# Cross-attention on one core: scores of four heads at once in every tile, and another split and order of the first stores

## The chip, the cores and the metric

One core of one Trainium2 chip. The metric is the time of one execution in microseconds on the device; a run's time is that of its slowest core, here the only one. "Span" is the time from the first to the last instruction in the profile of one execution.

## The reference, cut to what matters

```
def _L0_xattn_ref(tgt, memory, Wq, Wk, Wv):          # tgt, memory: (32, 512, 512) f32; NH = 16, dk = 32
    q = (tgt @ Wq.T).reshape(B, N, NH, dk).transpose(0, 2, 1, 3)
    k = (memory @ Wk.T)...                           # in the same way
    v = (memory @ Wv.T)...
    scores = jnp.einsum('bhqd,bhkd->bhqk', q, k) * (1.0 / np.sqrt(dk))
    probs = jax.nn.softmax(scores, axis=-1)
    att = jnp.einsum('bhqk,bhkd->bhqd', probs, v).transpose(0, 2, 1, 3).reshape(B, N, D)
    return tgt + att[0]
```

Only att of the first of the 32 sequences is used, and it is added to all 32. So the attention is computed once (512 queries, 512 keys, 16 heads of width 32), while 33.5 MB of x are read and 33.5 MB of sums are written.

## The kernel before

The 512 query rows are four tiles of 128. A row of x in SBUF is laid out in pairs: x is seen as two halves J of 256 rows, and partition p of a half holds rows 2p and 2p+1, r = 0 and 1. Tiles 0 and 1 are r = 0 and 1 of half 0, tiles 2 and 3 those of half 1. The 32 sequences are 16 groups g of two, and `slots` has 17 places of one group and one half (1 MB each). Half 0 is loaded into 16 of them while the weights and keys are prepared, group 0 of half 1 into the last. Every other group of half 1 (`slot_of`) goes into a place from which half 0's result has been stored.

**Adding and storing.** Tile 0 comes out in two units: FIRST is its first eight heads (columns 0 to 255), SECOND its other eight. Groups below SPLIT are added and stored in halves, once for each unit, those from SPLIT on as a whole row, in SECOND. Tile 1 is the unit ROW_1. Tiles 2 and 3 are added together at the end (`add_whole`, L698, on VectorE; L270 on GpSimd), one slot of 1 MB at a time. GpSimd has the odd groups of each unit and VectorE the even ones. VectorE's adds are written out by hand between the operations of the heads (L706 to L731, L751 to L780). All DMAs are issued by SyncE from one queue in the order L207 to L247: loads, FIRST's stores in the order of g, SECOND's stores in the order of g, BY_ROWS reloads of row 0 (`reload_row`, L191), then ROW_1's stores alternating with reloads, then `store_slot` for 16 groups. A store waits for its add (L182, L187), a reload for its slot's stores (L193). The stores of L188 need att of tiles 2 and 3, thus the end of the whole attention.

**The attention of one tile.** For every head h: TensorE makes the scores (3 passes, f32 split in a high and a low fp32r part) into PSUM bank h % 4; VectorE takes the negated maximum (`head_max`, L656); ScalarE takes the exponential with its sum (`exponent`, L574) into `probs[h % 2]`; TensorE turns it in four 128x128 transposes (`turn_probs`, L366) into PSUM bank 4 + h % 2; ScalarE copies that to `probs_t[h % 6]` (`copy_transposed`, L581). For every four heads TensorE multiplies with v (`weigh_values`, L375, 32 matmuls), VectorE copies the result (`copy_att_t`, L668) and inverts the sums (L661). At a tile's end `turn_back` (L387, L394) turns att back and `normalize` (L672) scales it.

A score matmul uses 32 of the 128 rows of the array, so the matmuls of different heads of a group of four go to different rows. `scores` (L347) issues pass by pass over the heads that it is given. In tile 0, and for heads 0 to 3 of every tile, these are four (`score_group`, L355, 12 matmuls), otherwise two (`score_pair`, L362, 6 matmuls). A group waits until all four heads before it have their exponentials, since the four banks are the same; a pair waits until the pair two before it has. One semaphore step, after the last matmul, releases all heads of one call.

Each engine works in the order in which its instructions are written. For tiles 1 to 3 these orders are `heads` of TensorE (L398), of ScalarE (L589) and of VectorE (L706). Between the heads of tile j they also prepare tile j+1: x is turned (`turn("x0_t")`), copied as a high part by ScalarE and a low part by VectorE (`empty`, L644), multiplied with wq in four chunks of three matmuls (`query_chunk`, L306), copied by ScalarE (`empty("q")`, L569), turned again (`turn("q_t")`) and copied in two parts. All of this uses PSUM bank 7, which the product with v uses too, and so chunk 0 waits for att of heads 0 to 3 to be copied away, and the turn of q for heads 4 to 7 (`pe.wait_ge(att_t_ready, ...)`). After tile 0 come `keep_warm` transposes (L459) on the identity.

## Time and profile before

| | |
|---|---|
| median of 3 runs | 195.05 us (194.85 to 198.45) |
| the profiled execution, its own time | 193.7 us |
| its span | 191.9 us |
| mean granted TensorE clock | 0.886 of full speed |
| busy: TensorE / VectorE / ScalarE / GpSimd | 129.7 / 113.5 / 96.3 / 63.6 us |
| moved by DMA | 71.5 MB, mean 373 GB/s |
| scores of heads 0 to 3 start in tile 0, 1, 2, 3 | 32.70, 67.68, 92.90, 118.95 us |
| last product with v starts | 142.40 us |
| first store of the last half is issued | 148.24 us |

Times in the profile are from the span's start. The profiled execution took 1.8 us more than its span. L with a number is a line of the kernel, "x12" a count of instructions, SPq SyncE's queue. A matmul's shown length includes the time until its result is there, so that matmuls in a row overlap in the timeline; the chain of waits shows how long they hold the engine.

### The profile page before, as it was taken

Reading aid. Unit: us, or ns where it says so; the run is one execution under the profiler, and the core shown is the slowest. Engines: PE = TensorE matmul, PEld = TensorE weight load, DVE = VectorE, ACT = ScalarE, POOL = GpSimd, SP = SyncE. Lnnn points to the kernel's source line nnn. Section 1 sums busy time; section 2 is a strip of 40 time slices with the busy share of each in tenths; the row PEclk is TensorE's granted clock in tenths of the full one; section 3 lists DMA queues with packets and bytes.
Section 4 is the critical chain, followed back from the end, with each engine's and each line's share of the span. In section 5 each row is a group of like instructions: output and inputs, shape, how many; then the busy total and the mean of one; then the engine's idle time right before and its main releaser. Section 6 shows DMA issues by size and latency. Waiting matters only on the chain.

```text
span 191.9 us, 3371 instructions
## 1 busy us (share of the span) xinstructions
PE 129.7 (68%) x1252; PEld 95.4 (50%) x1252; DVE 113.5 (59%) x169; ACT 96.3 (50%) x225; POOL 63.6 (33%) x33
## 2 busy tenths in 40 slices
PE   6999999999779967998879998888871000000000
PEld 6878786766547744766656765665650000000000
DVE  0546637653476578857599867945518999940000
ACT  2525553864677259868788879798860000000000
POOL 1000000000066599200079996000007999900000
PEclk9999999999999999999999999999999555555555
DMA  5999999999999793789999999999999999999997
GB/s 215 359 374 417 408 410 410 410 405 408 412 361 329 232 333 126 279 318 348 395 385 400 365 397 408 401 406 406 418 413 414 394 409 404 406 406 408 406 408 304
DMA packets 28976, 71.52 MB, mean 373 GB/s; under 512 B 1696, under 2 KB 6816, under 8 KB 28832
## 3 DMA queue, kind: packets, MB, share of 16 engines
q1 hardware_dynamic: 28960, 71.31, 96.5%
q8 instruction: 10, 0.16, 0.3%
q14 instruction: 6, 0.05, 0.1%
HBM read 37.75 MB, written 33.55 MB: 372 GB/s over the span
## 4 chain that ended last, share of the span: by engine, by line
PE 50%; ACT 16%; DVE 13%; issue 8%; DVEq 2%; POOL 0%; ACTq 0%; POOLq 0%
PE bank L371 11%; DVE slots L703 10%; ACT probs L578 8%; PE bank L351 7%; PE bank L329 6%; PE bank L306 6%; ACT probs_t L586 6%; PE bank L340 6%; PE bank L382 5%; PE bank L298 5%; PE bank L454 2%; DVE neg_max L658 2%; DVEq L58 2%; PE bank L394 1%; ACT ctx_t L572 1%
## 5 line engine op out<-in xcount | busy, mean ns | idle before, releaser
L264 POOL TENSOR_TENSOR slots<-slots,att_rows 128x1024 f32<-128x1024 f32 (+1 forms) x22 | 40.4, 1876 | 76.4 <-DVE att_rows L684 76.4
L578 ACT ACTIVATE probs<-bank,neg_max 128x512 f32<-128x512 f32 x64 | 45.1, 705 | 13.7 <-DVE neg_max L658 12.8
L658 DVE TENSOR_REDUCE neg_max<-bank 128x1 f32<-128x512 f32 x64 | 41.6, 680 | 15.7 <-PE bank L351 15.6
L371 PE MATMUL bank<-ident,probs 128*128 128x128 f32 x256 | 40.1, 282 | 8.7 <-ACT probs L578 7.4
L586 ACT COPY probs_t<-bank 128x512 f32<-128x512 f32 x64 | 37.7, 593 | 11.9 <-PE bank L371 10.3
L371 PEld LDWEIGHTS bank<-ident,probs 128*128 128x128 f32 x256 | 27.9, 140 | 23.3 <-ACT probs L578 19.1
L270 POOL TENSOR_TENSOR slots<-slots,att_rows 128x2048 f32<-128x2048 f32 x5 | 22.5, 4531 | 27.1 <-DVE att_rows L684 27.1
L351 PE MATMUL bank<-k_t,x_q 32*128 32x512 f32 x192 | 24.1, 424 | 0.9 <-issue 0.6
L703 DVE TENSOR_TENSOR slots<-slots,bank 128x2048 f32<-128x2048 f32 x11 | 24.3, 2279 | 0.0
L695 DVE TENSOR_TENSOR slots<-slots,bank 128x512 f32<-128x512 f32 (+1 forms) x20 | 18.7, 944 | 0.1
L382 PE MATMUL bank<-probs_t,v 128*32 128x128 f32 x512 | 17.3, 276 | 1.1 <-ACT probs_t L586 0.7
L351 PEld LDWEIGHTS bank<-k_t,x_q 32*128 32x128 f32 x192 | 12.3, 183 | 7.2 <-issue 5.4
L382 PEld LDWEIGHTS bank<-probs_t,v 128*32 128x32 f32 x512 | 13.0, 109 | 5.1 <-issue 2.2
L670 DVE COPY att_t<-bank 128x128 f32<-128x128 f32 x16 | 4.6, 289 | 17.4 <-PE bank L382 17.3
L306 PE MATMUL bank<-wq_t,x_q 128*128 128x512 f32 x48 | 14.3, 416 | 0.1
L578 ACT ACTIVATION_READ_ACCUMULATOR probs<-bank,neg_max 128x1 f32 x64 | 13.7, 214 | 0.0
L329 PE MATMUL bank<-ctx_t,wk_t 128*128 128x512 f32 x48 | 13.3, 409 | 0.4 <-ACT ctx_t L572 0.3
L340 PE MATMUL bank<-wv_t,ctx_t 128*128 128x512 f32 x48 | 13.3, 409 | 0.3 <-issue 0.3
L340 PEld LDWEIGHTS bank<-wv_t,ctx_t 128*128 128x128 f32 x48 | 8.3, 188 | 2.9 <-issue 1.1
L329 PEld LDWEIGHTS bank<-ctx_t,wk_t 128*128 128x128 f32 x48 | 8.3, 189 | 2.4 <-ACT ctx_t L572 0.6
L306 PEld LDWEIGHTS bank<-wq_t,x_q 128*128 128x128 f32 x48 | 8.0, 189 | 1.6 <-issue 0.7
L653 DVE TENSOR_TENSOR wk_t<-bank,wk_t 128x512 fp32r<-128x512 f32 x4 | 2.8, 692 | 10.1 <-ACT wk_t L572 10.1
(41 smaller groups left out, 89.5 us busy)
## 6 DMA issues: line engine op xcount, KB each, us to landing
slots<-in_x_dram SPq DMA_DIRECT2D x21, 1024.0 KB, 14.3
out_dram<-slots SPq DMA_DIRECT2D x16, 1024.0 KB, 13.3
slots<-in_x_dram SPq DMA_DIRECT2D x22, 512.0 KB, 9.0
out_dram<-slots SPq DMA_DIRECT2D x22, 512.0 KB, 7.0
out_dram<-slots SPq DMA_DIRECT2D x20, 256.0 KB, 3.1
ctx_raw<-in_ctx_dram SPq DMA_DIRECT2D x1, 1024.0 KB, 4.9
wq_raw<-in_L_xattn_Wq_dram SPq DMA_DIRECT2D x1, 1024.0 KB, 9.3
wv_raw<-in_L_xattn_Wv_dram SPq DMA_DIRECT2D x1, 1024.0 KB, 12.3
```

The lines of the kernel that those rows point to most:

```text
L264: nc.gpsimd.tensor_tensor(xs, xs, a.unsqueeze(1).to_broadcast([P, BPS, a.shape[1]]), ALU.add).then_inc(added[g], 1)
L270: nc.gpsimd.tensor_tensor(xs, xs, last_att.unsqueeze(1).to_broadcast([P, BPS, ROWS * D]), ALU.add).then_inc(added[g], 1)
L306: last = mm(job_bank("q", j), x0_q[:, j % 2, c, a, :], wq_t[:, c, b, :], start=(c == 0 and (a, b) == PASSES[0]), stop=(c == C - 1 and (a, ...
L329: last = mm(job_bank("k_t", g), wk_t[:, c, a, g * P:(g + 1) * P], ctx_t[:, c, b, :], start=(c == 0 and (a, b) == PASSES[0]), stop=(c == C ...
L340: last = mm(job_bank("v", t), ctx_t[:, c, a, t * P:(t + 1) * P], wv_t[:, c, b, :], start=(c == 0 and (a, b) == PASSES[0]), stop=(c == C - ...
L351: last = mm(bank[:, h % S_BANKS, :], x0_q[rows, j % 2, g, a, :], k_t[rows, g, b, :], start=((a, b) == PASSES[0]), stop=((a, b) == PASSES[-1]))
L371: last = nc.tensor.transpose(bank[:, PT_BANK + h % 2, t * P:(t + 1) * P], probs[:, h % 2, t * P:(t + 1) * P], ident[:, :])
L382: last = mm(att_t_ps[i * DK:(i + 1) * DK, g, :], v[:, t, h * DK:(h + 1) * DK], probs_t[:, (j * HEADS + h) % PT_SLOTS, t, :], start=(t == 0 ...
L578: nc.scalar.activation(probs[:, h % 2, :], bank[:, h % S_BANKS, :], ACT.Exp, bias=neg_max[:, h:h + 1], scale=1.0, accum_out=row_sum[:, h:h ...
L586: nc.scalar.copy(probs_t[:, (j * HEADS + h) % PT_SLOTS, :, :], bank[:, PT_BANK + h % 2, :].rearrange("p (t n) -> p t n", t=T)).then_inc(pr ...
L658: nc.vector.tensor_reduce(neg_max[:, h:h + 1], bank[:, h % S_BANKS, :], AX_X, ALU.max, negate=True).then_inc(max_ready, 1)
L703: nc.vector.tensor_tensor(xs, xs, back.unsqueeze(1).to_broadcast([P, BPS, ROWS * D]), ALU.add).then_inc(added[g], 1)
```

## The change

The stores of FIRST and SECOND go in an order written out by hand (`STORE_ORDER`); twelve groups instead of ten are added and stored in halves; twelve instead of ten have their row 0 reloaded by itself, before ROW_1's stores. `score_pair` goes: heads 4 to 15 of tiles 1 to 3 also have their scores made in groups of four. TensorE's, ScalarE's and VectorE's orders in `heads` are laid out again around this, and VectorE makes four of SECOND's adds instead of three before tile 1's heads.

```
-    SPLIT = 10
-    BY_ROWS = 10
-    DVE_GROUPS = {FIRST: (0, 2, 4, 6, 8), SECOND: (0, 2, 4, 6, 8, 10, 12, 14), ROW_1: (0, 2, 4, 6, 8, 10, 12)}
-    POOL_GROUPS = {FIRST: (1, 3, 5, 7, 9), SECOND: (1, 3, 5, 7, 9, 11, 13, 15),
+    SPLIT = 12
+    BY_ROWS = 12
+    DVE_GROUPS = {FIRST: (0, 2, 4, 6, 8, 10), SECOND: (0, 2, 4, 6, 8, 10, 12, 14), ROW_1: (0, 2, 4, 6, 8, 10, 12)}
+    POOL_GROUPS = {FIRST: (1, 3, 5, 7, 9, 11), SECOND: (1, 3, 5, 7, 9, 11, 13, 15),
                    ROW_1: (1, 3, 5, 7, 9, 11, 13, 14, 15)}
+    STORE_ORDER = {FIRST: (1, 0, 3, 2, 5, 4, 7, 6, 9, 8, 11, 10),
+                   SECOND: (0, 2, 1, 4, 3, 6, 5, 7, 9, 8, 11, 10, 12, 13, 14, 15)}
...
         def scores_through(j, h):
-            if j == 0:
-                return h // HPG + 1
-            return HG + (j - 1) * (PAIRS - 1) + (1 if h < HPG else h // PAIR)
+            return j * HG + h // HPG + 1
...
-            for g in range(SPLIT):
-                store(FIRST, g)
-            for g in range(GROUPS):
-                store(SECOND, g)
+            for unit in (FIRST, SECOND):
+                for g in STORE_ORDER[unit]:
+                    store(unit, g)
...
-            def score_pair(j, pair):
-                pe.wait_ge(exp_ready, j * HEADS + pair * PAIR - PAIR)
-                scores(j, range(pair * PAIR, (pair + 1) * PAIR))
-
...
                 turn_probs(j, 0)
                 turn_probs(j, 1)
-                score_pair(j, 2)
                 turn_probs(j, 2)
+                score_group(j, 1)
                 turn_probs(j, 3)
-                score_pair(j, 3)
-                turn_probs(j, 4)
-                turn_probs(j, 5)
                 if more:
                     emptied(pe, "x0_t", j + 1)
                 weigh_values(j, 0)
-                score_pair(j, 4)
-                turn_probs(j, 6)
+                turn_probs(j, 4)
                 if more:
                     pe.wait_ge(att_t_ready, j * HG + 1)
                     query_chunk(j + 1, 0)
+                turn_probs(j, 5)
+                if more:
+                    query_chunk(j + 1, 1)
+                turn_probs(j, 6)
+                score_group(j, 2)
                 turn_probs(j, 7)
                 if more:
-                    query_chunk(j + 1, 1)
-                score_pair(j, 5)
+                    query_chunk(j + 1, 2)
+                    query_chunk(j + 1, 3)
                 turn_probs(j, 8)
-                if more:
-                    query_chunk(j + 1, 2)
-                turn_probs(j, 9)
-                if more:
-                    query_chunk(j + 1, 3)
-                score_pair(j, 6)
                 if more:
                     raw_queries_out(j + 1)
                 weigh_values(j, 1)
+                turn_probs(j, 9)
                 turn_probs(j, 10)
+                score_group(j, 3)
+                turn_probs(j, 11)
                 if more:
                     pe.wait_ge(att_t_ready, j * HG + 2)
                     turn_queries(j + 1)
-                turn_probs(j, 11)
-                score_pair(j, 7)
                 turn_probs(j, 12)
                 turn_probs(j, 13)
                 if more:
                     emptied(pe, "q_t", j + 1)
                 weigh_values(j, 2)
                 turn_probs(j, 14)
+                if more:
+                    score_group(j + 1, 0)
                 turn_probs(j, 15)
-                if more:
-                    score_group(j + 1, 0)
                 weigh_values(j, 3)
...
             def heads(j):                                    # ScalarE
                 for h in range(HEADS):
                     exponent(j, h)
-                    if h > 0:
+                    if h % HPG > 0:
                         copy_transposed(j, h - 1)
+                    if h % HPG == HPG - 1:
+                        copy_transposed(j, h)
                     if j + 1 < T:
                         if h == 2:
                             empty("x0_t", j + 1)
-                        if h == 10:
+                        if h == 7:
                             empty("q", j + 1)
-                        if h == 11:
+                        if h == 12:
                             empty("q_t", j + 1)
-                copy_transposed(j, HEADS - 1)
...
                 for h in range(HPG, HEADS):                  # VectorE
                     if h % HPG == 0 and h >= 2 * HPG:
                         copy_att_t(j, h // HPG - 2)
+                    if h == HPG and j + 1 < T:
+                        empty("x0_t", j + 1)
+                    head_max(j, h)
                     if h == HEADS - 2 and j + 1 < T:
                         empty("q_t", j + 1)
-                    head_max(j, h)
-                    if h == HPG + 1 and j + 1 < T:
-                        empty("x0_t", j + 1)
...
-            add(SECOND, DVE_GROUPS[SECOND][0])
-            add(SECOND, DVE_GROUPS[SECOND][1])
+            for g in DVE_GROUPS[SECOND][:3]:
+                add(SECOND, g)
             empty("q_t", 1)
-            add(SECOND, DVE_GROUPS[SECOND][2])
+            add(SECOND, DVE_GROUPS[SECOND][3])
             for h in range(HPG):
                 head_max(1, h)
-            heads(1, SECOND, list(DVE_GROUPS[SECOND][3:]))
+            heads(1, SECOND, list(DVE_GROUPS[SECOND][4:]))
```

## Rows read from the trace of the kernel before

**Rows 1.** The page, 40 slices of 4.8 us: granted TensorE clock (tenths), data rate.

```profile
PEclk9999999999999999999999999999999555555555
...
GB/s 215 359 374 417 408 410 410 410 405 408 412 361 329 232 333 126 279 318 348 395 385 400 365 397 408 401 406 406 418 413 414 394 409 404 406 406 408 406 408 304
```

**Rows 2.** Timeline from 143 us: start, length, engine, line, operation, count. The end.

```profile
142.40 1.08 PE L382 MATMUL bank<-probs_t,v 128*32 128x128 f32 x32 [0.68 <-ACT probs_t L586]
...
143.90 0.66 PE L394 MATMUL bank<-ident,att_t 128*128 128x128 f32 x4 [0.42 <-DVE att_t L670]
...
148.24 28.70 SPq L188 DMA_DIRECT2D out_dram<-slots  x16
```

**Rows 3.** Chain of waits: start, length on the engine, what. Tile 2.

```profile
102.96 1.01 PE bank L382 x32
103.97 0.89 PE bank L351 x6
...
106.14 0.44 PE bank L371 x4
106.58 0.69 PE bank L306 x3
```

**Rows 4.** Timeline of tile 0: two score groups in a row.

```profile
39.25 0.97 PE L351 MATMUL bank<-k_t,x_q 32*128 32x512 f32 x12
...
45.76 0.97 PE L351 MATMUL bank<-k_t,x_q 32*128 32x512 f32 x12 [0.32 <-ACT probs L578]
```

**Rows 5.** Timeline at the change from tile 1 to tile 2.

```profile
92.90 0.97 PE L351 MATMUL bank<-k_t,x_q 32*128 32x512 f32 x12
93.00 0.59 ACT L586 COPY probs_t<-bank 128x512 f32<-128x512 f32 x1
...
93.80 1.08 PE L382 MATMUL bank<-probs_t,v 128*32 128x128 f32 x32
...
95.46 0.66 PE L394 MATMUL bank<-ident,att_t 128*128 128x128 f32 x4 [0.58 <-DVE att_t L670]
...
96.39 1.04 PE L371 MATMUL bank<-ident,probs 128*128 128x128 f32 x8
...
97.50 0.69 ACT L578 ACTIVATE probs<-bank,neg_max 128x512 f32<-128x512 f32 x1
...
98.34 0.66 PE L371 MATMUL bank<-ident,probs 128*128 128x128 f32 x4
98.65 0.61 ACT L572 CAST x_q<-bank 128x512 fp32r<-128x512 f32 x1
...
99.12 0.72 ACT L578 ACTIVATE probs<-bank,neg_max 128x512 f32<-128x512 f32 x1
```

**Rows 6.** Timeline at the change from tile 2 to tile 3.

```profile
118.95 0.98 PE L351 MATMUL bank<-k_t,x_q 32*128 32x512 f32 x12
...
119.86 1.08 PE L382 MATMUL bank<-probs_t,v 128*32 128x128 f32 x32
119.97 1.29 DVE L658 TENSOR_REDUCE neg_max<-bank 128x1 f32<-128x512 f32 x2 [1.45 <-PE bank L351]
```

**Rows 7.** Timeline of tile 2: an add, a turn and its copy, the last query chunk.

```profile
103.16 1.21 DVE L695 TENSOR_TENSOR slots<-slots,bank 128x1024 f32<-128x1024 f32 x1
...
104.29 0.28 DVE L670 COPY att_t<-bank 128x128 f32<-128x128 f32 x1
...
104.79 0.66 PE L371 MATMUL bank<-ident,probs 128*128 128x128 f32 x4
...
105.48 0.59 ACT L586 COPY probs_t<-bank 128x512 f32<-128x512 f32 x1 [0.90 <-PE bank L371]
...
109.62 0.93 PE L306 MATMUL bank<-wq_t,x_q 128*128 128x512 f32 x3
```

**Rows 8.** Timeline of tile 1's first heads.

```profile
67.68 0.97 PE L351 MATMUL bank<-k_t,x_q 32*128 32x512 f32 x12 [0.57 <-issue]
...
73.05 0.72 ACT L578 ACTIVATE probs<-bank,neg_max 128x512 f32<-128x512 f32 x1
```

More of the change, by code:

```diff
@@ L32, in cross_attention_add @@
     SLOTS = GROUPS + 1
-    PAIR = 2
-    PAIRS = HEADS // PAIR
     S_BANKS = 4
@@ L446, in heads @@
                 turn_probs(j, 14)
-                turn_probs(j, 15)
                 if more:
                     score_group(j + 1, 0)
+                turn_probs(j, 15)
                 weigh_values(j, 3)
```

## The prediction

> **What bounds the kernel now.** I read the data rate first, then the end of the timeline, then the chain of waits, then the timeline of single heads.
>
> The rate [rows 1] stands near 408 GB/s from the fourth slice to the eleventh and again from about slice 24 on. Between them are eight slices (361, 329, 232, 333, 126, 279, 318, 348) that fall short of 410 by 954 in all, so 954/410 x 4.8 = 11.2 us of transfer time are lost there. This is all that an earlier or better ordered store can win; a part of it is not idle time but slower small pieces.
>
> The end [rows 2] shows a second bound. The last product with v starts at 142.40; 5.84 us later, at 148.24, the first store of the last half is issued. Behind it lie 16 stores of 1 MB, 16.8 MB, which at the 406 GB/s of the last slices take 41.3 us, and the span ends at 191.9. These stores can't start before the attention of all four tiles is done. From 142.40 to the end are 49.5 us that nothing in the change touches. So the attention's chain and the data rate meet at about 148: if only the transfers before it get better, the queue runs dry and waits for the attention; if the attention gets later, the end gets later one for one, and whatever the stores won is lost. The attention decides, and the question is how long tiles 1 to 3 take. Now their score groups start at 67.68, 92.90 and 118.95 [rows 8, 5, 6]: 25.2 us, 26.05 us, and 23.45 us from the last to 142.40.
>
> **The change part by part.**
>
> *Splits and store order.* SPLIT 12 moves two half adds (a half add is two times shorter than the row add of 1.13 us, 103.16 to 104.29 [rows 7]) into tile 0's time, where VectorE waits for TensorE anyway, and two in GpSimd, which waits for att; the order lets the first store go about 1 us sooner and takes away the wait at SECOND's seventh store. I bound the gain for the transfers by 0 and 11.2 us and take 4. On the path that sets the end it is 0, since the attention ends later (below). SyncE's queue has four more issues (two stores, two reloads), about 0.5 us each, long before 148. More small pieces cost transfer time that has become free. Bounds for this part: 0, or 1 us lost. I take 0.
>
> *TensorE's work.* A pair holds TensorE for 0.89 us [rows 3], a group for 0.91 (118.95 to 119.86, [rows 6]). Six pairs a tile become three groups: 6 x 0.89 - 3 x 0.91 = 2.6 us less for TensorE a tile, 7.8 us in three tiles. It counts only where TensorE is what everything waits for.
>
> *The loop that a group makes.* Steps from rows: scores start to first maximum 1.02, two maxima in 1.29, so 0.6 to 0.65 each [rows 6]; exponential to its turn, or to the scores that wait for it, 0.84 (97.50 to 98.34), exponential and a copy on ScalarE 1.15 and a copy 0.47 (97.50, 98.65, 99.12), so an exponential alone 0.68 [rows 5]; turn to copy 0.69 (104.79 to 105.48, [rows 7]); a turn holds TensorE 0.44, a query chunk 0.69, a product with v 1.01 [rows 3]; a copy's start to the product that waits for it 0.80 (93.00 to 93.80, [rows 5]); that product to TensorE's next, through the copy of att, 1.50 (142.40 to 143.90, [rows 2]), of which the copy has 0.28 [rows 7].
>
> With S the start of a group's scores, the new order runs so: the turn of the last head of the group before starts at S+0.91, because it stands behind the scores; its copy at S+1.60; the group's first exponential stands behind that copy, at S+2.07 (its maximum would allow S+1.7); second S+2.75; third, behind the first turn's copy, S+4.5; fourth S+5.7; the next scores S+6.5. So a group takes at least 6.1 (2.93 between its neighbours' exponentials and 3.15 for its own four), and about 6.5 with a product with v in it. Tile 0 works so already and shows 6.51 (39.25 to 45.76, [rows 4]). A pair lets ScalarE go on at 1.15 a head while the next scores are made; a group drains it each time. Four groups are 24.3 to 26 us where tile 3 takes 23.45 now.
>
> *Stall at query chunk 0 (tiles 1, 2).* It now stands before turn 5 and waits for att of heads 0 to 3. That copy stands on VectorE behind the maxima of heads 4 to 7 and two adds: S1 + 1.02 + 4 x 0.60 + 2 x 1.13 + 0.09 (the reciprocal) = S1+5.77; with 0.35 for the copy and the step to TensorE the chunk starts at S1+6.12, turn 5 at 6.81, its copy at 7.50, exponential 7 at 7.97, the next scores at S1+8.8 instead of 6.5. Queued behind the waiting chunk are turns 5 and 6 and with them ScalarE. Cost 2.3 us a tile. Before, a pair of scores and a turn lay in front of the chunk and nothing waited.
>
> *q copied after head 7 (tiles 1, 2).* Chunks 2 and 3 follow turn 7: chunk 3 starts at S2 + 0.91 + 0.44 + 0.69 = 2.04, its result is there 0.93 later (the matmuls of 109.62, [rows 7]), ScalarE's copy of q is at S2+3.0, and exponential 8 stands behind it: S2+3.5 instead of 2.07. Group 2 to group 3 is then 7.8. In group 3 q_t stands between exponentials 12 and 13, but chunk and maxima are in time: 6.3 to the next tile's scores.
>
> *Change of tile.* Scores of the next tile now come before turn 15. Turn 15's copy is at S0+1.60, the last product with v at S0+2.4 (it was S0+0.91), turned back 1.50 later, at S0+3.9, and from there as now: turn 0 at +0.93 (95.46 to 96.39), exponential 2 at +1.11, x0's copy and exponential 3 at +1.15 and +0.47 [rows 5], S1 = S0+8.4. In tile 3 there is no x0: S0+7.4.
>
> *Sum.* Tile 1, whose start has no such change (scores at 67.68, exponential 3 at 73.05, S1 at 73.9 [rows 8]): 6.2 + 8.9 + 7.8 + 6.3 = 29.2, now 25.2: +4.0. Tile 2: 8.4 + 8.8 + 7.8 + 6.3 = 31.3, now 26.05: +5.3. Tile 3: 7.4 + 6.5 + 6.4 + 7.5 (to its last product with v) = 27.8, now 23.45: +4.4. Together +13.7. By 162 the transfers before will be done, so the first stores find an empty queue; now about 0.5 MB (1.2 us) of loads are still ahead of them, while an empty queue needs some time to start: I take -0.5. Span 191.9 + 13.7 - 0.5 = 205.1; the profiled execution took 1.8 us more than its span: 206.9, say 207. That stands to its own 193.7; the median shown is 1.35 higher, and I leave that in the range.
>
> The Trainium skill (TensorEngine Tiling (Array Packing), PSUM Bottleneck) says that row tiling speeds up TensorE but not the emptying of PSUM, which may then be the bottleneck. That is this case: the exponentials and maxima of [rows 5, 6] are the same for a pair and a group.
>
> **Rivals.**
>
> *TensorE is the bound, and this is faster.* For it: in tile 2 the chain of waits lies on TensorE for long stretches, pairs and chunks back to back, between 102 and 111 us [rows 3]. If TensorE never waits under the new order, tiles 1 to 3 are 7.8 us shorter, the stores fill that much of the 11.2 us, and the time is 193.7 - 7.8 = 185.9. It decides where TensorE has work whenever it could take it. Against it: tile 3 has no query chunks and still takes 23.45, and 16 heads at 1.15 make 18.4, so the loop between the engines sets the time there, and the change makes that loop longer. The Trainium skill (TensorE: Matmul & The Clock Gate, Part 3: Packing small matmuls — row/col tiling) gives four row tiles with 512 columns a measured 3.07 times speed, which speaks for this rival; the durations in [rows 3, 6] agree that four heads take the time of two.
>
> *Only the group loop costs.* The waits at chunk 0 and q hide (the chunk's wait is met earlier than I have it, q's copy falls in a gap): then tile 1 is 6.2 + 6.5 + 6.4 + 6.3 = 25.4, tile 2 27.6, tile 3 27.8: +0.2, +1.6, +4.4 = +6.2, time 199.4. For it: tile 0's 6.51 with value chunks in between. Against it: the order is fixed on every engine.
>
> *No measurable difference.* The slack between exponentials and scores is smaller than the steps say and the change of tile costs nothing: +0 to +3, time 194 to 197.5.
>
> *TensorE's clock.* The row of the granted clock [rows 1] has it in full, 2.4 GHz, through slice 31 (to 149), and at 1.2 GHz after; the last matmuls stand at 143.90 [rows 2]. The gaps that I foresee are at most 2.3 us. If it falls in a tile, TensorE's 19 us of work there grow by up to as much: 213 to 226.
>
> **How the numbers follow.** Forecast 0.62, only the group loop 0.20, no difference 0.08, TensorE bound and faster 0.06, clock 0.04. About 2% (3.9 us) is what a measurement of this kernel can tell from no change. Slower: 0.62 + 0.20 + 0.04 = 0.86; within 2%: 0.08; faster: 0.06. The forecast's own range is 202 to 211 (half of either stall gone, or half a microsecond more in each group). The range 198 to 213 takes in the second case and leaves out the others.
>
> **What would show it.** Score groups of tiles 2 and 3 start near 97 and 128, the last product with v near 156, the first store of the last half near 162. ScalarE waits for VectorE's maximum before heads 4, 8, 12; TensorE waits about 2 us for VectorE's copy of att (L670's successor) once a tile in tiles 1 and 2; the rate is near 400 through slices 13 to 18 and has a hole of 5 to 15 us before the last stores. I am wrong if the score groups are 26 us apart or less, or if the hole is missing.

## The result and the profile after

The changed kernel takes 209.97 us (median of 4 runs, 209.35 to 210.33), the kernel before 196.75 (4 runs, 194.85 to 198.59). The ratio is 1.0767, 95% interval 1.0714 to 1.0821: slower. (Before's median includes executions near 198 at a lower mean clock, which the ratio leaves out.) Forecast were 207.0 us, range 198 to 213, and slower with 0.86. The profiled execution took 209.63 us with a span of 207.8.

| | before | forecast | after |
|---|---|---|---|
| tile 1, from its first scores to tile 2's (us) | 25.2 | 29.2 | 30.74 |
| tile 2, the same to tile 3's | 26.05 | 31.3 | 32.16 |
| tile 3, to the last product with v | 23.45 | 27.8 | 27.69 |
| last product with v starts | 142.40 | 156 | 158.56 |
| first store of the last half | 148.24 | 162 | 164.40 |
| from the last product with v to the end | 49.5 | 49.0 | 49.2 |

First the page of the changed kernel, granted clock and data rate, 40 slices of 5.2 us each (before: [rows 1]):

```profile
PEclk9999999999999997999985999999999655555555
...
GB/s 235 359 385 415 408 410 409 412 397 392 402 333 271 342 174 276 49 303 394 386 388 337 350 360 401 403 408 406 417 307 5 80 398 401 400 404 404 405 407 330
```

Three things are new. Slices 29 to 31 (307, 5, 80), from 151 to 166 us, are the hole that was forecast: all earlier transfers are done and the last stores can't start. And the clock falls below full in slices 15, 20 and 21, in tiles 1 and 2; before it was full until the attention was over. And the transfers of slices 11 to 17 haven't become better but worse: they fall short of 410 GB/s by 1122 in all, 14.2 us of transfer time against 11.2 before, with a second hole in slice 16 (49, near 86 us). The forecast had the rate near 400 there.

The end, answering to [rows 2]: start, length, engine, line.

```profile
158.56 1.08 PE L373 MATMUL bank<-probs_t,v 128*32 128x128 f32 x32 [0.68 <-ACT probs_t L573]
...
160.06 0.66 PE L385 MATMUL bank<-ident,att_t 128*128 128x128 f32 x4 [0.41 <-DVE att_t L659]
...
164.40 4.76 SPq L184 DMA_DIRECT2D out_dram<-slots  x4
```

1.50 us from the product to the turn and 5.84 to the first store, both as before; only the place has moved, by 16.2 us. The span grew by 15.9.

The group loop as it runs in tile 3, group 2, where no work for a next tile lies in it (timeline, compare the tile 0 groups of [rows 4]):

```profile
144.62 0.97 PE L346 MATMUL bank<-k_t,x_q 32*128 32x512 f32 x12 [0.50 <-ACT probs L565]
...
145.53 0.66 PE L362 MATMUL bank<-ident,probs 128*128 128x128 f32 x4
...
145.65 1.89 DVE L647 TENSOR_REDUCE neg_max<-bank 128x1 f32<-128x512 f32 x3 [3.66 <-PE bank L346]
...
146.22 0.58 ACT L573 COPY probs_t<-bank 128x512 f32<-128x512 f32 x1 [1.18 <-PE bank L362]
...
146.71 0.69 ACT L565 ACTIVATE probs<-bank,neg_max 128x512 f32<-128x512 f32 x1
...
151.15 0.97 PE L346 MATMUL bank<-k_t,x_q 32*128 32x512 f32 x12 [0.92 <-ACT probs L565]
```

Read it as the forecast's steps: the turn of head 7 at S+0.91, its copy at S+1.60, after ScalarE has stood for 1.18 us, exponential 8 at S+2.09, the next group at S+6.53. VectorE had waited 3.66 us for these scores. This is a loop in which each of the three engines stands once a group. ScalarE's exponential comes right behind its copy, without a wait for VectorE's maximum; what ScalarE waits for is TensorE's turn, which stands behind the twelve score matmuls.

The stall at query chunk 0, in tile 1:

```profile
78.34 0.58 ACT L573 COPY probs_t<-bank 128x512 f32<-128x512 f32 x1 [0.41 <-PE bank L362]
...
78.89 1.21 DVE L684 TENSOR_TENSOR slots<-slots,bank 128x1024 f32<-128x1024 f32 x1
...
80.02 0.28 DVE L659 COPY att_t<-bank 128x128 f32<-128x128 f32 x1
80.36 1.45 PE L301 MATMUL bank<-wq_t,x_q 128*128 128x512 f32 x3 [2.05 <-DVE att_t L659]
81.61 1.05 PE L362 MATMUL bank<-ident,probs 128*128 128x128 f32 x4
...
82.70 0.59 ACT L573 COPY probs_t<-bank 128x512 f32<-128x512 f32 x1 [3.09 <-PE bank L362]
...
84.41 0.98 PE L346 MATMUL bank<-k_t,x_q 32*128 32x512 f32 x12
```

VectorE adds a whole row (78.89) in front of the copy of att (80.02), TensorE waits 2.05 us for that copy with the chunk, turn 5 comes behind the chunk (81.61), and ScalarE has waited 3.09 us for turn 5. The forecast had the chunk at S1+6.12; it is at 80.36 - 74.20 = 6.16. What the forecast didn't have is the length of the chunk: its three matmuls hold TensorE 1.25 us (80.36 to 81.61) instead of 0.69. Windows of 1 us (busy time of PE, PEld, DVE, ACT, POOL, then granted clock, DMA share, GB/s) show why:

```profile
79.00:80.00 1.00, 0.00 (x0) 0.00 (x0) 1.00 (x1) 0.61 (x2) 0.00 (x0) 1.00 0.77 256
80.00:81.00 1.00, 0.64 (x2) 0.54 (x3) 0.30 (x2) 0.00 (x0) 0.00 (x0) 0.80 0.00 0
81.00:82.00 1.00, 1.00 (x4) 0.70 (x4) 0.00 (x0) 0.00 (x0) 0.00 (x0) 0.50 1.00 360
...
83.00:84.00 1.00, 1.00 (x5) 0.70 (x4) 0.00 (x0) 0.97 (x3) 0.00 (x0) 0.50 0.76 277
84.00:85.00 1.00, 1.00 (x15) 0.74 (x14) 0.00 (x0) 0.48 (x1) 0.00 (x0) 0.99 0.06 16
```

The clock drops from 2.4 to 1.2 GHz within 80 to 81 and is back at 84. In tile 2 it is low from 107.9 to 114.8, and there TensorE waits only 0.23 us for att's copy, because its own slower work comes late; the chunk starts at 113.05, 6.09 us behind the scores of 106.96, at the same place.

The copy of q, in tile 2:

```profile
116.57 0.97 PE L346 MATMUL bank<-k_t,x_q 32*128 32x512 f32 x12 [0.21 <-ACT probs L565]
...
117.89 1.64 PE L301 MATMUL bank<-wq_t,x_q 128*128 128x512 f32 x6
...
119.56 0.60 ACT L556 ACTIVATE att_rows<-bank 128x512 f32<-128x512 f32 x1 [0.81 <-PE bank L301]
...
120.06 0.68 ACT L565 ACTIVATE probs<-bank,neg_max 128x512 f32<-128x512 f32 x1
```

Exponential 8 stands behind q at S2+3.49; the forecast said S2+3.5.

### The profile page after: what moved, and what is told of

The parts are those of the page before. It is cut to its first block, busy times and chain, and to the rows that moved or that the text cites. A ratio compares the mean times of both kernels' runs of the same rounds, so it can differ in the third digit from the quotient of the medians.

```text
span 207.8 us, 3378 instructions
## 1 busy us (share of the span) xinstructions
PE 127.4 (61%) x1252; PEld 94.8 (46%) x1252; DVE 113.5 (55%) x170; ACT 97.4 (47%) x225; POOL 63.7 (31%) x34
## 3 DMA queue, kind: packets, MB, share of 16 engines
q1 hardware_dynamic: 30048, 71.31, 90.6%
## 4 chain that ended last, share of the span: by engine, by line
PE 49%; DVE 15%; ACT 14%; issue 9%; DVEq 2%; POOL 0%; ACTq 0%; POOLq 0%
PE bank L362 11%; DVE slots L692 10%; ACT probs L565 8%; PE bank L346 7%; PE bank L301 6%; PE bank L373 6%; PE bank L324 6%; PE bank L335 5%; ACT probs_t L573 4%; PE bank L293 4%; DVE neg_max L647 2%; PE bank L441 2%; DVE slots L684 2%; DVEq L59 2%; PE bank L385 1%
## 5 line engine op out<-in xcount | busy, mean ns | idle before, releaser
L259 POOL TENSOR_TENSOR slots<-slots,att_rows 128x512 f32<-128x512 f32 (+1 forms) x23 | 40.5, 1802 | 83.2 <-DVE att_rows L673 83.2
L362 PE MATMUL bank<-ident,probs 128*128 128x128 f32 x256 | 41.4, 290 | 15.4 <-ACT probs L565 14.5
L565 ACT ACTIVATE probs<-bank,neg_max 128x512 f32<-128x512 f32 x64 | 44.4, 696 | 11.7 <-DVE neg_max L647 10.7
L362 PEld LDWEIGHTS bank<-ident,probs 128*128 128x128 f32 x256 | 29.2, 146 | 30.1 <-ACT probs L565 20.3
L373 PE MATMUL bank<-probs_t,v 128*32 128x128 f32 x512 | 18.1, 285 | 4.9 <-ACT probs_t L573 4.5
L346 PE MATMUL bank<-k_t,x_q 32*128 32x512 f32 x192 | 15.6, 425 | 6.9 <-ACT probs L565 6.2
L373 PEld LDWEIGHTS bank<-probs_t,v 128*32 128x32 f32 x512 | 13.8, 113 | 8.4 <-issue 4.5
L301 PE MATMUL bank<-wq_t,x_q 128*128 128x512 f32 x48 | 15.7, 458 | 2.4 <-DVE att_t L659 2.3
L346 PEld LDWEIGHTS bank<-k_t,x_q 32*128 32x128 f32 x192 | 8.1, 183 | 11.1 <-ACT probs L565 8.3
L301 PEld LDWEIGHTS bank<-wq_t,x_q 128*128 128x128 f32 x48 | 9.1, 209 | 4.9 <-DVE att_t L659 2.9
```

The source lines that it names most:

```text
L259: nc.gpsimd.tensor_tensor(xs, xs, a.unsqueeze(1).to_broadcast([P, BPS, a.shape[1]]), ALU.add).then_inc(added[g], 1)
L301: last = mm(job_bank("q", j), x0_q[:, j % 2, c, a, :], wq_t[:, c, b, :], start=(c == 0 and (a, b) == PASSES[0]), stop=(c == C - 1 and (a, ...
L346: last = mm(bank[:, h % S_BANKS, :], x0_q[rows, j % 2, g, a, :], k_t[rows, g, b, :], start=((a, b) == PASSES[0]), stop=((a, b) == PASSES[-1]))
L362: last = nc.tensor.transpose(bank[:, PT_BANK + h % 2, t * P:(t + 1) * P], probs[:, h % 2, t * P:(t + 1) * P], ident[:, :])
L373: last = mm(att_t_ps[i * DK:(i + 1) * DK, g, :], v[:, t, h * DK:(h + 1) * DK], probs_t[:, (j * HEADS + h) % PT_SLOTS, t, :], start=(t == 0 ...
L565: nc.scalar.activation(probs[:, h % 2, :], bank[:, h % S_BANKS, :], ACT.Exp, bias=neg_max[:, h:h + 1], scale=1.0, accum_out=row_sum[:, h:h ...
```

## The experiments

Three theories were open. The forecast's: the attention's new order costs all of it, in the group loop, the two stalls and the change of tile. The rivals: the stores and splits carry a part; or TensorE's saved time shortens the tiles. The fall of the clock came with the result and had to be priced.

**The stores alone.** Edit on the kernel before: `SPLIT`, `BY_ROWS` 12, `STORE_ORDER` and its adds.

> The kernel before with only the first part of the change: STORE_ORDER, SPLIT and BY_ROWS 12, the adds that go with them; the attention's order as before. Theory (the attention sets the end): last product with v stays near 142.4 and the first store of the last half near 148.2; the transfers win about 4 us of their holes in slices 13 to 18, which come back as a hole of about that size before 148; time within 1 us of before. Rival (the transfers set the end): the end comes 4 us sooner, about 190 us.

Measured: 194.74 us (10 runs) beside 195.68, ratio 0.996, interval 0.992 to 1.000. The profiled execution's last product with v is at 142.55 and its first last store at 148.39. The transfers did win their time, and lost it again ahead of the last stores (windows of 2 us, DMA share and GB/s last):

```profile
144.00:146.00 2.00, 0.66 (x4) 0.42 (x4) 1.26 (x2) 0.00 (x0) 0.49 (x1) 1.00 0.95 383
146.00:148.00 2.00, 0.00 (x0) 0.00 (x0) 1.97 (x2) 0.00 (x0) 2.00 (x1) 1.00 0.24 98
148.00:150.00 2.00, 0.00 (x0) 0.00 (x0) 2.00 (x2) 0.00 (x0) 2.00 (x2) 0.62 0.37 152
150.00:152.00 2.00, 0.00 (x0) 0.00 (x0) 2.00 (x2) 0.00 (x0) 2.00 (x2) 0.50 1.01 395
```

Against a full share, 0.1 + 1.6 + 1.3 us = 3 us stand empty. The part gains at most 1% and costs nothing.

**The scores alone.** Edit on the changed kernel: the stores, splits and adds of before.

> The changed kernel with the stores, splits and adds of the kernel before; only the attention's new order is left of the change. Theory: all of the loss is here, time within 1 us of the changed kernel (209 to 211), last product with v near 158.5. Rival (the splits or the store order carry a part of the loss): 2 us or more below the changed kernel.

Measured: 210.11 us (4 runs), ratio to before 1.076, interval 1.068 to 1.084, beside 1.0767 for the whole change. All of the loss is in the attention's order. In its tile 2 the clock stays full, and the stall at chunk 0 is there by itself:

```profile
107.02 0.97 PE L345 MATMUL bank<-k_t,x_q 32*128 32x512 f32 x12 [0.98 <-ACT probs L564]
...
113.09 0.97 PE L300 MATMUL bank<-wq_t,x_q 128*128 128x512 f32 x3 [1.98 <-DVE att_t L658]
```

The chunk starts at S1+6.07 after a wait of 1.98 us, and from group 1 to group 2 it is 8.84 us.

**Tile 3 alone in groups**, the rest in pairs, the change of tile as before. TensorE's part of the edit; ScalarE's order in tile 3 is that of the changed kernel.

```
+                if not more:
+                    for h in range(HEADS):
+                        if h % HPG == HPG - 1 and h < HEADS - 1:
+                            score_group(j, h // HPG + 1)
+                        turn_probs(j, h)
+                        if h in (3, 8, 13, 15):
+                            weigh_values(j, (3, 8, 13, 15).index(h))
+                    return
```

> The kernel before, but tile 3 alone has its scores in groups of four (TensorE's and ScalarE's order in tile 3 as in the changed kernel); its first group still stands behind turn 15 of tile 2. No query chunk and no x0 lie in tile 3, so this is the group loop by itself. Theory: from tile 3's first scores to its last product with v 26.5 us instead of 23.45 (6.2 + 6.5 + 6.5 + 7.4), time +3 us, about 198. Rival (TensorE's freed 2.6 us shorten the tile): 21 to 22 us, time 193 or unchanged.

Measured: 197.92, 202.0, 202.01 and 203.04 us. The profiled execution (203.04):

```profile
123.78 0.97 PE L353 MATMUL bank<-k_t,x_q 32*128 32x512 f32 x12
...
129.95 0.97 PE L353 MATMUL bank<-k_t,x_q 32*128 32x512 f32 x12 [0.50 <-ACT probs L588]
...
136.36 0.98 PE L353 MATMUL bank<-k_t,x_q 32*128 32x512 f32 x12 [0.50 <-ACT probs L588]
...
144.44 0.97 PE L353 MATMUL bank<-k_t,x_q 32*128 32x512 f32 x12 [0.92 <-ACT probs L588]
...
151.85 1.08 PE L384 MATMUL bank<-probs_t,v 128*32 128x128 f32 x32 [0.68 <-ACT probs_t L596]
```

6.17, 6.41, 8.08 and 7.41 us where 6.2, 6.5, 6.5 and 7.4 were expected; the third has 1.6 us too much, and in its window 140 to 142 the clock is granted at 0.50. Without that the tile is 26.5, 3.0 us more than in pairs. So the loop alone costs a tile 3 us, and TensorE's 2.6 us of freed time buy nothing. The clock can fall in tile 3 too once it runs in groups. But only 4.6 us of this execution's time are in tile 3. The rest is in tiles 1 and 2, which run in pairs as in the kernel before: the clock was low from 71.0 to 81.3 and from 105.2 to 108.6, and they took 28.18 and 27.28 us instead of 25.22 and 26.05. So the fall of the clock isn't peculiar to the groups.

**A fill at the chunk's wait.**

```
                 turn_probs(j, 4)
                 if more:
+                    for _ in range(18):
+                        nc.tensor.transpose(bank[:, PT_BANK + 1, 0:P], ident[:, :], ident[:, :])
                     pe.wait_ge(att_t_ready, j * HG + 1)
```

> The changed kernel with 18 transposes of the identity (2.0 us of TensorE) into the free bank 5 just before query chunk 0's wait in tiles 1 and 2, where TensorE idles about 2 us. Theory: the granted clock stays at 2.4 GHz in 81 to 84 and in 108 to 114 us, tile 1 becomes 1.3 us shorter (29.4) and tile 2 0.8 us (31.4), time 2 us less, 208. Rival (the transposes do not keep the clock, or the slower matmuls were not what the loop waited for): unchanged, 210.

Measured: 208.7 in one run, 212.8 to 213.5 in three. My expectation failed: the clock fell nevertheless, and earlier. The windows of its profiled execution (213.49 us):

```profile
70.00:72.00 2.00, 0.98 (x7) 0.75 (x8) 1.93 (x4) 1.75 (x5) 2.00 (x3) 1.00 1.03 345
72.00:74.00 2.00, 0.99 (x8) 0.51 (x5) 0.04 (x1) 2.00 (x6) 2.00 (x2) 1.00 1.03 345
74.00:76.00 2.00, 1.34 (x12) 0.74 (x12) 0.65 (x1) 1.08 (x3) 2.00 (x2) 0.71 0.32 112
76.00:78.00 2.00, 1.24 (x8) 0.71 (x4) 1.76 (x3) 0.72 (x2) 1.53 (x1) 0.50 0.00 0
```

The clock fell at 74.8, 8 us ahead of the chunk (83.15). The wait at the chunk isn't what made it fall here. TensorE had worked 0.98 and 0.99 us of the two windows of 2 us before; but the changed kernel had the same two windows (1.31 and 0.66 us), kept the full clock in them and lost it only at 80.6. With the clock low, turn 4 came at 79.99 instead of 77.65, and the fill behind it held the chunk until 83.15, where att's copy (81.03) would have let it go at 81.4. The one execution at 208.7 has a mean clock of 0.883 against 0.846 to 0.855 of the others and is what the theory expected; why it was spared isn't known.

**A fill wherever TensorE waits.** Edit on the changed kernel, for tiles 1 and 2, each into the bank that the next turn will write:

```
+            def fill(j, h, times):
+                pe.wait_ge(probs_t_ready, j * HEADS + h - 1)
+                for _ in range(times):
+                    nc.tensor.transpose(bank[:, PT_BANK + h % 2, 0:P], ident[:, :], ident[:, :])
...
+                if j == 1:
+                    fill(j, 0, 8)
                 turn_probs(j, 0)
                 turn_probs(j, 1)
+                if more:
+                    fill(j, 2, 4)
                 turn_probs(j, 2)
+                if more:
+                    fill(j, 3, 6)
                 score_group(j, 1)
                 turn_probs(j, 3)
                 if more:
+                    fill(j, 4, 6)
...
                 turn_probs(j, 4)
+                if more:
+                    fill(j, 5, 18)
```

> The changed kernel with transposes of the identity wherever TensorE waits in the first half of tiles 1 and 2: 8 in front of tile 1's turn 0, 4 in front of turn 2, 6 in front of group 1's scores, 6 in front of the first product with v, 18 in front of query chunk 0, each in the bank that the next turn will write. Theory (the clock falls because TensorE has had too little work in the whole stretch before, not in the one gap at chunk 0): the clock stays at 2.4 GHz, tile 1 is 29.4 and tile 2 31.4, time about 208. Rival (transposes of the identity do not count as work for the clock): it falls as before, 210 to 213.

Measured: 208.63 us (208.51 to 209.22, 3 runs). The same windows, and tile 1's groups:

```profile
70.00:72.00 2.00, 1.85 (x16) 1.40 (x13) 2.00 (x4) 1.45 (x4) 2.00 (x2) 1.00 1.04 345
72.00:74.00 2.00, 1.96 (x14) 1.40 (x14) 0.29 (x1) 1.94 (x5) 2.00 (x3) 1.00 1.03 348
74.00:76.00 2.00, 1.71 (x20) 1.06 (x19) 0.69 (x1) 1.45 (x4) 2.00 (x2) 1.00 0.37 128
```

```profile
68.79 0.97 PE L346 MATMUL bank<-k_t,x_q 32*128 32x512 f32 x12 [0.58 <-issue]
75.02 0.97 PE L346 MATMUL bank<-k_t,x_q 32*128 32x512 f32 x12 [0.29 <-ACT probs L578]
83.93 0.97 PE L346 MATMUL bank<-k_t,x_q 32*128 32x512 f32 x12 [0.23 <-ACT probs L578]
91.84 0.98 PE L346 MATMUL bank<-k_t,x_q 32*128 32x512 f32 x12 [0.92 <-ACT probs L578]
98.23 0.97 PE L346 MATMUL bank<-k_t,x_q 32*128 32x512 f32 x12
```

The clock is full throughout tiles 1 to 3 of the profiled execution (208.51; the mean clock of the three is 0.897, 0.889 and 0.884, against 0.860 to 0.866 of the changed kernel). Tile 1 is 6.23 + 8.91 + 7.91 + 6.39 = 29.44 us, tile 2 31.41, tile 3 27.70, within 0.25 of the forecast's 29.2, 31.3 and 27.8. So the forecast's sum was the sum at full clock, and the fall of the clock costs the profiled execution of the changed kernel 1.3 us in tile 1 and 0.75 in tile 2. (The fill itself costs the loop nothing: tile 2 of the run with the scores alone, at full clock without a fill, took 31.39.)

**Query chunk 0 behind turns 5 and 6.**

```
                 turn_probs(j, 4)
-                if more:
-                    pe.wait_ge(att_t_ready, j * HG + 1)
-                    query_chunk(j + 1, 0)
                 turn_probs(j, 5)
-                if more:
-                    query_chunk(j + 1, 1)
                 turn_probs(j, 6)
+                if more:
+                    pe.wait_ge(att_t_ready, j * HG + 1)
+                    query_chunk(j + 1, 0)
                 score_group(j, 2)
                 turn_probs(j, 7)
                 if more:
+                    query_chunk(j + 1, 1)
                     query_chunk(j + 1, 2)
```

> The changed kernel with query chunk 0 of the next tile behind turns 5 and 6, in front of the scores of heads 8 to 11, and chunks 1 to 3 behind turn 7. Theory (the chunk's wait for VectorE's copy of att stops turns 5 and 6, and slower matmuls follow): from group 1 to group 2 6.8 us instead of 10.2 (tile 1) and 9.6 (tile 2); q comes 0.7 later, so group 2 to 3 8.6 instead of 7.9; net 4.5 to 5 us less, about 205. Rival (VectorE's maxima hold the loop there and the chunk's place is indifferent): unchanged, 210.

Measured: 207.78 us (2 runs, ratio 1.070, interval 1.063 to 1.076). Tile 2's groups:

```profile
106.96 0.97 PE L346 MATMUL bank<-k_t,x_q 32*128 32x512 f32 x12 [0.99 <-ACT probs L564]
...
113.95 0.97 PE L346 MATMUL bank<-k_t,x_q 32*128 32x512 f32 x12
...
122.55 0.97 PE L346 MATMUL bank<-k_t,x_q 32*128 32x512 f32 x12 [0.92 <-ACT probs L564]
```

6.99 where 6.8 was expected and 8.84 is the price of the old place at full clock; then 8.60 where 8.6 was expected. The stall is shown, at 1.9 us in the one tile that had the full clock (2.3 forecast). The total is 2.8 us too high against the expectation: in tile 1 the clock fell at its group 1 (74.7 us), and that step took 9.15.

**Chunk and q.** On top of the last: q copied behind head 9, turn 9 in front of the product with v.

```
-                        if h == 7:
+                        if h == 9:
                             empty("q", j + 1)
...
                 turn_probs(j, 8)
+                turn_probs(j, 9)
                 if more:
                     raw_queries_out(j + 1)
                 weigh_values(j, 1)
-                turn_probs(j, 9)
```

> As the run with chunk 0 moved, and besides ScalarE's copy of q behind head 9 instead of head 7, turn 9 in front of the product with v of heads 4 to 7. Theory: group 2 to group 3 is 6.7 us instead of 8.6, tile 1 26.1, tile 2 28.2, tile 3 unchanged at 27.7, so 8.6 us less than the changed kernel, 201.4; what is left over the kernel before, some 6 us, is the group loop and the change of tile. Rival (the group loop costs nothing, the two stalls were all): 195.

Measured: 204.51 to 206.71 us (3 runs). Group 2 to 3 is 7.07 in both tiles (forecast 6.7). Tile 1 is 27.75, tile 2 30.91 and tile 3 27.25; the clock fell in both and took group 1 to 2 to 8.06 and 9.20. With 6.99 there they would be 26.7 and 28.7. The rival (195) is out: with both stalls gone, the kernel is still 6% slower than before (1.060, interval 1.052 to 1.068), and without the 3.3 us of the two falls its three tiles would still be 7.9 us longer than before.

**The change of tile.** On top of that, the next tile's first scores behind turn 15 again.

> As the run with chunk 0 and q moved, and the next tile's first scores behind turn 15 again, as before the change. Theory: the first scores come 0.4 later, but the last product with v no longer waits for turn 15's copy, so first to second score group is 7.1 instead of 8.3 in tile 2 and 6.2 instead of 7.3 in tile 3: 1.5 us less in all. Rival (the order at the change of tile is indifferent): unchanged within 0.5 us.

Measured: 203.4 and 207.84 us, too far apart to tell anything by the time. The lengths tell it: first to second group 7.10 (tile 2) and 6.17 (tile 3) against 8.26 and 7.33, and the group before it 6.98 against 6.38. So 1.16 won and 0.6 lost at each of two places, 1.1 us in all (1.5 expected). The profiled execution, 207.84, had the clock at 1.2 GHz in three stretches (76.6 to 80.0, 103.9 to 114.2, 134.6 to 148.3).

With this the loss at full clock can be shared out. With the fill the three tiles are 13.8 us longer than before (88.55 against 74.7). Moving chunk 0 and q takes 5.9 of that away (with 6.99 put in for the two steps that the clock had lengthened), the change of tile 1.1. The 6.8 us that stay are left to the group loop, which tile 3 by itself showed at 3.0 us.

**Early rows.** The first experiment left a hole in front of the last stores. If transfers and attention meet there, it takes both to get below the kernel before. Edit: row 0 of groups 0, 1 and 3 of the last half is added in tile 3 (it needs tile 2's att only) and stored ahead; at the end these groups need row 1.

```
+            for g in EARLY:                       # (0, 1, 3)
+                store_early(g)
             for g in range(GROUPS):
                 store_slot(g)                     # row 1 alone for g in EARLY
...
-            heads(3, None, [])
+            heads(3, None, list(EARLY))           # each behind an odd head's maximum
```

Without the new stores:

> The kernel before, but row 0 (tile 2's att) of groups 0, 1 and 3 of the last half is added on VectorE during tile 3 and stored ahead of the last stores; at the end these three need row 1 only. 1.5 MB, 3.9 us of stores, leave the tail and the first store of the tail can go 1.1 us sooner. Theory (before, transfers and attention meet at 148, so neither alone can shorten it): within 1 us of before. Rival (only the tail behind the attention counts): 4 us less, 191.

Measured: 195.1 us (9 runs, 194.07 to 197.83), ratio 1.000, interval 0.995 to 1.005. The profiled execution is one of the longer ones (197.18). Its tiles 1 and 2 run in pairs in the order of the kernel before, and the clock falls in them (tile 1's first scores and its next two pairs; before, a pair took 0.96):

```profile
68.40 0.97 PE L364 MATMUL bank<-k_t,x_q 32*128 32x512 f32 x12 [0.57 <-issue]
...
72.72 1.65 PE L364 MATMUL bank<-k_t,x_q 32*128 32x512 f32 x6
...
76.19 1.65 PE L364 MATMUL bank<-k_t,x_q 32*128 32x512 f32 x6
```

The clock is low from 71.2 to 81.4 and from 105.3 to 108.7; tile 1 takes 28.2 us instead of 25.2 and tile 2 27.3 instead of 26.05.

With the new stores:

> The same early rows 0 on top of the run with the new store order and splits, pairs of scores kept. The transfers there have a hole of 3 us at 146 to 150. Theory: the early rows fill it, first store of the tail near 147, 3 us less than before, about 192. Rival (VectorE's three adds delay tile 3's maxima by as much, or the rate is lower with small pieces): no gain.

Measured: 191.72 us (190.78 to 193.53, 6 runs), ratio 0.990, interval 0.983 to 0.997. Its profiled execution (190.78, span 188.9) has no hole any more, and the first store of the tail goes at 147.04:

```profile
GB/s 213 368 361 417 410 409 410 409 406 408 410 409 318 270 344 342 226 318 369 393 383 396 366 386 405 404 407 403 404 420 411 406 418 419 423 420 418 418 418 207
```

```profile
147.04 1.50 SPq L197 DMA_DIRECT2D out_dram<-slots  x2
```

0.996 and 1.000 alone, 0.990 together: that is what two limits that meet look like. By the times alone it isn't shown, since the intervals of 0.996 and 0.990 overlap; the traces say it, with a hole of 3 us ahead of the last stores in the one and none in the other. The changed kernel's stores are worth something, if its scores are left in pairs.

**The same with a fill in tile 1** (8 transposes in front of turn 0, 6 in front of turn 3), and the kernel before with that fill alone.

> The run with new stores and early rows 0, pairs of scores, and in tile 1 8 transposes of the identity in front of turn 0 and 6 in front of turn 3. Theory: where that kernel's slower executions (193.5) had the clock fall in tile 1, these do not, so all are near 191. Rival: the fill does not hold the clock, spread as before, 191 to 193.5, or the fill delays the turns and costs 0.5.

Measured: 191.26 us (191.14 to 191.72, 4 runs), ratio 0.982, interval 0.975 to 0.989. Its median is the lowest of all kernels here, 0.5 us under the same kernel without the fill, whose fastest execution (190.78) is below all of its own.

> The kernel before with nothing but the 14 transposes of the identity in tile 1 (8 in front of turn 0, 6 in front of turn 3). Theory (some executions of the kernel before take about 198 because the clock falls in tile 1, and the fill holds it): all executions near 194 to 195.5, none at 198, the median about 1 us or more under that of before in the same rounds. Rival (the 198 has another cause): executions at 198 remain.

Measured: 194.81 us (10 runs) beside 195.07, ratio 0.998, interval 0.995 to 1.002, and two of the ten at 198.1. The theory failed: this fill doesn't remove the 198s. These executions have a lower mean clock (0.861 and 0.862 against 0.878 to 0.886), and none of them was profiled. The two traces of kernels with the same order in tiles 1 and 2 and such a mean clock (0.857 with early rows alone, 0.846 with tile 3 in groups) lost 3.0 us in tile 1 and 1.2 in tile 2 by falls that began at 71 and 105 us, which is about the distance from 194 to 198. So the theory on the cause fits, and it is the remedy that fails: 14 transposes in tile 1 don't keep every execution from it. Where the clock fell in these two isn't recorded. Whether the fill helps the best kernel, or its four runs were lucky, stays open.

## Why the prediction was right, point by point

- *The attention sets the end.* Shown. 142.40 to the end was 49.5, is 49.2 now, and the end moved by 15.9 as the last product with v moved by 16.2. The first experiment won 3 us of transfer time for at most 1% of the time.
- *Stores and splits: 0.* Right (0.996, touching 1.000), and the run with the scores alone reproduces the whole loss. The 4 us that I took as the transfers' gain are there in pairs (3 us). In the changed kernel the transfers ahead of the last stores stand 14.2 us short against 11.2 instead; with the scores alone it is 16.2 in the same slices. That the adds, which stand between the later heads, hold the stores up is likely and not shown. Nothing hung on it, because the attention sets the end.
- *The group loop.* Right. Its steps are in the profile to 0.1 us, and tile 3 alone in groups is 3.0 us longer (6.17 + 6.41 + 6.5 + 7.41 at full clock).
- *Query chunk 0.* The wait is where and as long as forecast (S1+6.16 against 6.12); the way from group 1 to 2 is 8.8 to 8.9 at full clock as forecast. Taken away, it gives 1.9 us, not 2.3, measured in one tile; that the chunk's new place costs the rest itself is my guess.
- *q behind head 7.* Right: exponential 8 at S2+3.49, group 2 to 3 7.92. Moved, it gives 1.5 us against the 8.60 that a later chunk needs, and 0.85 against the changed kernel.
- *Change of tile.* Forecast 8.4 and 7.4 for the first step, measured 8.25 and 7.34; the experiment prices it at 0.6 a tile net.
- *Sum.* 13.7 forecast, 16.2 measured. 2.05 of the difference is the clock, 0.3 a later start of tile 1 (67.97 against 67.68), and 0.2 small steps. For the empty queue I took -0.5; the way from the last product to the end is 49.2 against 49.5, so -0.3.
- *The step that failed: the rival on the clock.* I gave it 0.04, on the ground that no gap would be over 2.3 us, priced it at 6 to 19 us, and so had it at 0 in the sum. It happened in the profiled execution of the changed kernel and in those of five of its six variants, and cost the first 2.05 us. Both halves were wrong. The longest gap doesn't tell: in the run with the fill at the chunk the clock fell at 74.8, and the longest wait of TensorE in the 6 us before was 1.0 us. Nor does a stretch in which TensorE is busy half of the time: it lay ahead of that fall, and the changed kernel went through the same stretch at full clock. With work in the small gaps too, the clock stayed full in the one execution profiled. What decides in a single execution these runs don't show, and pairs of scores don't rule it out. The price was too high because a fall lasts 3 to 14 us here, and because in it part of the loop is waiting for ScalarE and VectorE anyway: in tile 1 it lasts 3.4 us and costs 1.3. So the forecast comes out 2.5 us low with every other step in place; that the range took it in is owed to the room left for something else.
- *Signs that didn't come.* ScalarE was to wait for VectorE's maximum before heads 4, 8 and 12. It waits 1.2 us for TensorE's turn of the head before instead, which is what the forecast's own steps say, and its exponential follows the copy at once (before head 8, the copy of q). The rate was to be near 400 in slices 13 to 18, and wasn't. The wait of 2 us for att's copy came in tile 1, and in tile 2 only where the clock was full.
- *TensorE is the bound, and faster.* This rival is out. TensorE's time was freed (its scores are 24.1 us busy before and 15.6 after, 2.8 a tile), and TensorE's waits grew by more: from tile 1's first scores to the last product with v it was busy 66.6 of 74.7 us before and 64.0 of 90.6 after, so it stands 26.6 us instead of 8.1. The Trainium skill (TensorE: Matmul & The Clock Gate, Part 3: Packing small matmuls — row/col tiling) says that matmuls in different row tiles run at the same time, with a measured 3.07 times speed for four. The trace agrees as far as it goes: the 12 matmuls of four heads take 0.97 us from first start to last end, the 6 of two heads 0.96; no run here makes one head's alone. Who waits for the result is another matter.

## What to carry to other kernels

Where several engines pass a head around, count how often the loop drains: packing more heads into one call of the fastest step makes the rest wait for one release, and saves time only on an engine that never waits. Before reordering, follow one lap of the loop with the steps' durations and put each moved instruction in its engine's queue: the stalls here were instructions standing in front of others (an add before a copy, a chunk before a turn, a copy before an exponential), and their sum for three tiles came out within 1% at full clock (88.3 against 88.55 us). Where transfers and a chain of work meet ahead of a fixed tail, shorten both, or move work out of the tail: each alone gave 0 to 0.4%, both together 1%, with intervals that still overlap.

## What was not expected of the hardware

TensorE's clock fell to 1.2 GHz in kernels whose TensorE was at work all the time in pieces: at 80.6 us in the changed kernel right behind a wait of 2.05 us, at 74.7 in the variant with the chunk moved, behind waits of 0.7 and 1.0 us. It came back 3 to 14 us later. It also fell in the old order, in pairs, behind a wait of 1.0 us (at 71.2 us with early rows alone). With transposes of the identity in all these gaps it stayed at 2.4 GHz in the profiled execution (busy 3.8 of the 4 us from 70 to 74). The same 4 us were half filled, 2.0 us, both in the run where it fell at 74.8 and in the changed kernel, where it didn't fall until 80.6. The Trainium skill (TensorE: Matmul & The Clock Gate, Part 4: PE-mode transpose) says that a transpose doesn't count as PE-busy in the same way. This case speaks against it for f32 transposes, weakly: one profile at full clock, three executions with a higher mean clock than the changed kernel's four, and beside them the fills that didn't hold the clock.

The fall differs from execution to execution of one kernel: tile 3 in groups gave 197.9 once and 202 to 203 three times on one chip. Kernels that differ by 2 us can't be told apart by single executions here. The lengths of their single steps at full clock can, since the same step agreed to 0.1 us over all runs.
